# A mixture-of-experts block on one core: x1 formed on VectorE in its own step, its squares on ScalarE, the expert choice one step sooner

## What is computed

```python
x = x + layernorm(A(layernorm(x)))      # A: long convolution (S4D), below
x = x + layernorm(F(layernorm(x)))      # F: mixture of experts, below
```

```python
z = layernorm(x) * g + b
logits = z @ rW + rb                    # 8 experts
top 2 of softmax(logits) -> weights w
hid = gelu(z @ W1[e] + b1[e]);  out = hid @ W2[e] + b2[e]
return z_in + sum_e w[e] * out[e]
```

## Time and profile before

| | us |
|---|---|
| median of 3 runs | 642.32 (641.46 to 644.99) |
| the profiled execution | 644.5 |
| its span | 642.9 |

### The profile page before, as it was taken

One profiled execution on the slowest core, in us unless ns is written; L12 is line 12 of the kernel. 1 busy time (PEld: TensorE's weight loads), 2 busy tenths in 40 slices (PEclk: granted clock), 3 DMA queues, 4 the chain that ended last, 5 costly groups with the idle time before them and its releaser, 6 DMA issues. The chain is left out here.

```text
span 642.9 us, 12334 instructions
## 1 busy us (share of the span) xinstructions
PE 484.8 (75%) x2809; PEld 418.0 (65%) x2810; DVE 488.9 (76%) x1426; ACT 329.3 (51%) x646; POOL 262.4 (41%) x205
## 2 busy tenths in 40 slices
PE   0479899848997773600189999999999999992970
PEld 0239888736876663600078888888888889892760
DVE  7997959889988977884057778777777787770796
ACT  6974721353455366620055555555555555545485
POOL 0001586545776665788503223322332323233420
PEclk9998999968987985555579999999999999995995
DMA  6106500100110657642432222222222222215963
GB/s 198 66 0 262 197 1 0 66 1 9 59 68 33 229 197 216 227 139 74 153 118 68 81 66 82 66 82 66 82 67 80 66 82 72 75 49 212 346 229 145
DMA packets 36826, 69.55 MB, mean 108 GB/s; under 512 B 7520, under 2 KB 23648, under 8 KB 36160
## 3 DMA queue, kind: packets, MB, share of 16 engines
q1 hardware_dynamic: 30320, 51.48, 24.3%
q0 software_dynamic: 6480, 17.77, 7.7%
HBM read 42.02 MB, written 27.21 MB: 108 GB/s over the span
## 5 line engine op out<-in xcount | busy, mean ns | idle before, releaser
L1165 POOL DMA_INDIRECT y_rows<-y_sb,dst x71 | 76.6, 1079 | 192.7 <-DVE y_sb L1056 149.9
L1340 PE MATMUL psum<-ws,z_hl 128*128 x426 | 119.8, 417 | 0.8 <-DVE z_hl L1033 0.8
L1359 PE MATMUL psum<-ws,h_hl 128*128 x852 | 116.0, 286 | 0.1
L1359 PEld LDWEIGHTS psum<-ws,h_hl 128*128 128x128 f32 x852 | 103.6, 189 | 0.3 <-issue 0.3
L1147 POOL DMA_INDIRECT z_rows<-zn,pos x64 | 76.9, 1201 | 30.6 <-issue 17.7
L1340 PEld LDWEIGHTS psum<-ws,z_hl 128*128 128x128 f32 x426 | 76.7, 192 | 16.0 <-issue 1.5
L591 ACT CAST h_hl<-psum 128x512 fp32r<-128x512 f32 x71 | 41.7, 587 | 75.8 <-PE psum L1349 75.8
L1041 DVE TENSOR_TENSOR hb<-psum,b1r 128x512 f32<-128x512 f32 x71 | 49.1, 691 | 37.5 <-issue 34.0
L583 ACT ACTIVATE z_f<-psum,gb 128x128 f32<-128x128 f32 x142 | 57.0, 452 | 32.8 <-PE psum L1327 31.1
L1232 PE MATMUL psum<-pm,ft 128*128 128x256 f32 x256 | 65.7, 418 | 0.4 <-DVE tmp L836 0.4
L1327 PE MATMUL psum<-ident,z_in 128*128 128x128 f32 x142 | 28.6, 284 | 43.9 <-DMA z_in<-z_rows 42.0
(11 more groups left out here) (200 smaller groups left out, 874.7 us busy)
## 6 DMA issues: line engine op xcount, KB each, us to landing
z_in<-z_rows SPq DMA_DIRECT2D x71, 129.0 KB, 2.1
w_raw<-in_dram SPq DMA_DIRECT2D x16, 512.0 KB, 4.9
ya<-y_rows SPq DMA_DIRECT2D x16, 512.0 KB, 6.1
xs<-in_dram SPq DMA_DIRECT2D x8, 512.0 KB, 5.4
x_dram<-xs SPq DMA_DIRECT2D x8, 512.0 KB
x1m<-x_dram SPq DMA_DIRECT2D x2, 2048.0 KB, 8.4
out_dram<-acc SPq DMA_DIRECT2D x8, 512.0 KB, 2.6
b1r<-in_dram SPq DMA_DIRECT2D x8, 256.0 KB
```

Of the source, the lines that this page charges most:

```text
L1165: pool.indirect_dma_start(y_rows, bass.IndirectOffsetOnAxis(ap=dst[q][:, 0:1], axis=0), y_sb[q][:, :], None).then_inc(sem(f"y_out{q}"), 16)
L1340: last = TE.matmul(ps_h[q], z_hl[q][:, a, k], w_at(e1, c, k * F, F), start=n == 0, stop=n == 5)
L1359: last = TE.matmul(ps_y[q], h_hl[q][:, a, k], w_at(e2, c, 1024 + k * H, H), start=n == 0, stop=n == 11)
```

## The change

- x1 is made on VectorE in the step of its o: four instructions compute `o * rs + x` with an accumulator output that gives the sum of each token (its mean follows from it). The shift of o (`-mean*rs`, the same for all channels of a token) is not added to x1. It doesn't change the norm of x1; it is kept in `xb` and added in the mix, in one more small VectorE instruction per row. `dl` and GpSimd's addition go away.
- The variance of x1 comes from four ScalarE instructions (Square with the mean as bias and an accumulator output) in the same step, instead of `bn_stats` and `bn_aggr` on VectorE one step later. ScalarE then makes `zn` in the same step too, and copies the token numbers.
- `turn`, the logits and `choose` come one step sooner (row n-2); the ranks, `place` and the scatters stay with row n-3, and for the last rows row 6 is placed in step 8 beside row 5. `place` now stands behind r's statistics. The router bias and the experts' first rows are added by matmuls with the identity instead of on VectorE.
- GpSimd: `combine(row, 1)` moves to the start of the next step, `combine(row, 0)` waits for o, and the eight scatters of a row are issued as five and three around it. GpSimd makes no weight splits any more.
- The splits of the weights are spread over other steps; only that of expert 7 stays behind the tile table.
- SyncE writes the padding blocks before it waits for the last scatters.
- A one-element Gelu is put on ScalarE ahead of the tiles.

```diff
@@ SyncE
             behind = [sp.value_load(padi[0:1, e:e + 1], min_val=0, max_val=ROWS - P) for e in range(E)]
-            for i in (2, 3):
-                sp.wait_ge(sem(f"scattered{i}"), 128)
             for e in range(E):
                 sp.dma_start(z_rows[bass.ds(behind[e], P), :], zpad[:, :]).then_inc(sem("pads"), 16)
...
             sp.wait_ge(sem("pads"), 16 * E)
+            for i in (2, 3):
+                sp.wait_ge(sem(f"scattered{i}"), 128)
             load_z(0, 0)
@@ ScalarE
-            def renormalise(mid):
-
-                sigma(mid, 3)
-                act.wait_ge(sem("st_x1"), mid.b + 1)
+            def renormalise(row):
+
+                act.wait_ge(sem("x1_mean"), row.b + 1)
+                for k in range(4):
+                    last = nc.scalar.activation(dump[:, k], xs[row.b][:, k], ACT.Square, bias=mv1[:, row.b, k, 0:1],
+                                                accum_out=mv1[:, row.b, k, 1:2])
+                last.then_inc(sem("var3"), 1)
+                sigma(row, 3)
+                act.wait_ge(sem("st_x1"), row.b + 1)
...
+                elif row.b < 6:
+                    act.wait_ge(sem(f"scattered{row.par}"), 64 * (row.b - row.par))
...
+                nc.scalar.copy(zn[buf(row.b)][:, :, H], tok[:, row.b])
...
+                for e in HIGH.get(n, ()):
+                    split_high(e)
                 if cur.live:
-
                     sigma(cur, 1)
-                    act.wait_ge(sem("st_o"), cur.b + 1)
-                    if not cur.first():
-                        act.wait_ge(sem("x1_ready"), cur.b)
-                    for k in range(4):
-                        last = nc.scalar.activation(dl[:, k], o[:, k], ACT.Identity, bias=rs[:, 1, 4 + k:5 + k],
-                                                    scale=rs[:, 1, k:k + 1])
-                    last.then_inc(sem("dl_ready"), 1)
                 if inv.live:
...
-                if mid.live and n != B:
-                    renormalise(mid)
-                for e in HIGH.get(n, ()):
-                    split_high(e)
+                if cur.live:
+                    renormalise(cur)
@@ VectorE
                     stats(lambda k: r[:, k], 2)
+                if last_tail.live and n != B + 1:
+                    place(last_tail)
                 if cur.live:
                     do(inverse(cur, 2))
...
                 if n == B:
-                    mid_now()
+                    choose(tail)
...
                 if nxt.live:
                     mult(nxt, 1)
+                if n == B:
+                    place(tail)
                 if cur.live:
                     do(inverse(cur, 1))
-                    V.scalar_tensor_tensor(rs[:, 1, 4:8], mv[1][:, :, 0], -1.0, rs[:, 1, 0:4], ALU.mult,
+                    V.scalar_tensor_tensor(xb[:, cur.b], mv[1][:, :, 0], -1.0, rs[:, 1, 0:4], ALU.mult,
                                            ALU.mult).then_inc(sem("st_o"), 1)
...
+                    for k in range(4):
+                        last = V.scalar_tensor_tensor(xs[cur.b][:, k], o[:, k], rs[:, 1, k:k + 1], xs[cur.b][:, k], ALU.mult,
+                                                      ALU.add, accum_out=st[:, 3, 0, k:k + 1])
+                    last.then_inc(sem("x1_ready"), 1)
+                    dve.wait_ge(sem("x1_ready"), cur.b + 1)
+                    V.tensor_scalar(mv1[:, cur.b, :, 0], st[:, 3, 0, 0:4], -1.0 / H, None, ALU.mult).then_inc(sem("x1_mean"), 1)
                 for e in LOW.get(n, ()):
                     split_low(e)
...
+                if tail.live and n != B:
+                    choose(tail)
+                if cur.live:
+                    do(inverse(cur, 3))
+                    V.tensor_tensor(rs[:, 3, 4:8], mv1[:, cur.b, :, 0], rs[:, 3, 0:4], ALU.mult).then_inc(sem("st_x1"), 1)
@@ VectorE, mix
                 V.scalar_tensor_tensor(rm[:, par, 2, :], mvm[par][:, :, 0], -1.0, rm[:, par, 1, :], ALU.mult,
-                                       ALU.mult).then_inc(sem("m_rs"), 1)
+                                       ALU.mult).then_inc(sem("m_sh"), 1)
+                dve.wait_ge(sem("m_sh"), b + 1)
+                gate(dve)
+                V.tensor_tensor(rm[:, par, 2, :], rm[:, par, 2, :], xb[:, bass.ds(back(b), 1)].rearrange("p a k -> p (a k)"),
+                                ALU.add).then_inc(sem("m_rs"), 1)
@@ GpSimd
+                nxt, cur, tail, last_tail = (Row(n, k) for k in (1, 0, -2, -LAG))
+
+                if cur.live and cur.b:
+                    if cur.b > 1:
+                        pool.wait_ge(sem("st_x1"), cur.b - 1)
+                    combine(cur, 1)
+                if last_tail.live and n != B + 1:
+                    scatter(last_tail, 0, 5)
                 if nxt.live:
+                    if nxt.b > 1:
+                        pool.wait_ge(sem("o_ready"), nxt.b - 1)
                     combine(nxt, 0)
-                    combine(nxt, 1)
+                    if nxt.b == 0:
+                        combine(nxt, 1)
+                if last_tail.live and n != B + 1:
+                    scatter(last_tail, 5, 8)
+                if n == B:
+                    scatter(tail, 0, 8)
@@
-HIGH = {3: (0,), 4: (1,), 5: (2,), 6: (3,), 7: (4,), 9: (5,), 10: (6,)}
-LOW = {9: (0,), 10: (1,), B + LAG: (4, 5, 6, 7)}
-LOW_POOL = {B + LAG: (2, 3)}
+HIGH = {0: (0, 1), 1: (2,), 4: (3,), 7: (4,), 8: (5, 6)}
+LOW = {1: (0, 1), 2: (2,), 8: (3,), 9: (4, 5, 6), B + LAG: (7,)}
```

More of the change, by code:

```diff
@@ L879, in place @@
                 V.tensor_copy(zn[buf(row.b)][:, :, H + 1], mif[:, 1])
-                V.tensor_copy(pos[row.par][:, :, :], posr[:, :, :]).then_inc(sem("pos_ready"), 1)
+                with nc.allow_low_precision(reason="one term of each sum is not zero, and it is a whole number"):
+                    V.tensor_reduce(pos[row.par][:, :, :], prod[:, :, :, :], AX.X, ALU.add).then_inc(sem("pos_ready"), 1)
             def step(n):
-                nxt, cur, mid, tail = (Row(n, k) for k in (1, -1, -2, -LAG))
@@ L896, in mid_now @@
-                def mid_now():
-                    dve.wait_ge(sem("x1_ready"), mid.b + 1)
-                    for k in range(4):
-                        last = V.bn_stats(st[:, 3, k, :], xs[mid.b][:, k])
-                    do(last)
-                    mid_statistics()
-                    mid_scales()
+                nxt, cur, tail, last_tail = (Row(n, k) for k in (1, -1, -2, -LAG))
                 if cur.live:
@@ L1124, in fold, with scatter @@
                 G.tensor_tensor(pm[b][:, 1], xn[b % 3][:, 0:2], xn[b % 3][:, 2:4], ALU.subtract).then_inc(sem("pm_ready"), 1)
-            def split_low(e):
-                pool.wait_ge(sem("w_high"), e + 1)
-                G.tensor_tensor(ws[:, e, 1], w_raw[e][:, :], ws[:, e, 0].bitcast(F32), ALU.subtract).then_inc(sem("w_low"), 1)
-            def step(n):
-                nxt, cur, tail = (Row(n, k) for k in (1, -1, -LAG))
+            def scatter(row, lo, hi):
+                pool.wait_ge(sem("pos_ready"), row.b + 1)
+                for i in range(lo, hi):
+                    pool.indirect_dma_start(z_rows, bass.IndirectOffsetOnAxis(ap=pos[row.par][:, i // 4, i % 4:i % 4 + 1], axis=0),
+                                            zn[buf(row.b)][:, i % 4], None).then_inc(sem(f"scattered{buf(row.b)}"), 16)
@@ L1153, in _ @@
             steps(step)
-            for e in LOW_POOL[B + LAG]:
-                split_low(e)
             def scatter_y(t, q):
```

130 lines of the change are left out of this document (44 added, 86 removed).

## The result

The changed kernel takes 622.18 us (median of four runs, 619.58 to 627.88), the kernel before 643.65 beside it (641.46 to 645.51): a ratio of 0.968, 95% interval 0.960 to 0.976. Forecast were 620 us, range 607 to 634. The profiled execution (627.88 us, span 626.3) is the slowest of the four, so one more profile of the same kernel was taken (a2_changed, span 620.3), and both stand in this table. The marks were read from the timelines: start of r in step 3 and step 8 on VectorE, end of the last scatter on GpSimd, first transpose of a tile on TensorE, first addition of the mix on VectorE, end. In brackets is what the prediction gave, put on the times of before.

A forecast was written before the change was run, and what follows sets the result against it. VectorE was taken to bound the steps, and waits for scatters and padding the gap before the tiles. -25.0 us to the first tile and +2.4 in the mix gave -22.6 on 642.3: 619.7, say 620 us, range 607 to 634.

The forecast's parts named there:

- Part 1, VectorE's loop: Full steps, 3 to 6: VectorE's own chain, with its wait for ScalarE's root, takes 19.4 us against 22.2.
- Part 1, TensorE's loop: Full steps: 17.6 us of TensorE work plus half-clock loss and following work; both loops meet at 20.2, saving 8.1 over four.
- Part 2: First and last steps: step 3 begins 3.1 us later, step 7 takes 17.4, step 8 begins at 237.1.
- rival 2: Full steps: zn waits for scatters now started in the same step; if 3 us per step, +12, 632 us; chance 0.12.
- Part 3: Last scatters: sixteen with 11.9 us of stalls end at 288.8 against 305.53, -16.7; row 7's own path just inside.
- The stall rule: Scatters: a VectorE weight split stops GpSimd's descriptor work; one costs about 1.8 to 2.1 us, four in a row 8.65.
- Part 4: Gap before the first tile: padding lands before the last scatter, saving 8.3 us; first transpose at 293.3, -25.0 in all.
- Part 5: Mix: one more small VectorE instruction per row costs 0.3 us, eight rows +2.4; bounds +0.2 and +6.
- GpSimd's placing: Full steps: sums moved away from o's shift save 1.1 us per step, lost again if GpSimd is a microsecond late.
- x1 at half rate: x1's four VectorE instructions run at two cycles per element: 1.07 us more per step, +8, 628 us; chance 0.2.
- Padding not the last: Before the first tile: weight loads, b1 and b2 or the table come last, the 8.3 us stay: 628; chance 0.07.
- TensorE's clock slower than before: Full steps: TensorE stays at half clock, 39 us per step, +19 in each of four, about 695 us; chance 0.03.

The follow-up runs named there:

- e3_rank_later: Changed kernel with TensorE's rank matmuls moved between the two halves of the forward transform: 618.33 us, 0.963 of the kernel before.
- b1_pads_alone: Kernel before with only the padding blocks issued ahead of the wait for the last scatters: 635.24 us, 0.987 of the kernel before.
- e6_both: e3_rank_later with ScalarE's copy of s moved behind the squares and root of x1's variance: 616.40 us, 0.956 of the kernel before.
- e10_loads_later: e6_both with expert 5's weight load and the x1 stores behind it held until row 3's scatters landed: 612.96 us, 0.953 of the kernel before.
- s1_sums_back: Changed kernel with both GpSimd sums at once, without their waits, and all eight scatters behind them: 657.88 us, 1.023 of the kernel before.
- s2_no_waits: Changed kernel with its GpSimd order kept and only the sums' waits for o and x1's scales removed: 636.71 us, 0.991 of the kernel before.
- e8_fill_half: e6_both with unused identity matmuls in TensorE's idle stretches from step 7 to the first tile and before the mix: 614.36 us, 0.953.

## Why the prediction was right, by its steps

**The sum.** -22.6 was forecast on the profiled span; a2_changed ends at 620.3, -22.6, and after at 626.3, -16.6. The ratio of the medians gives -3.2%, 20.6 us, on 642.3. The range held all four runs. That a2_changed agrees to the tenth is luck, for several terms were off and cancelled. Against the forecast it has 2.9 us less in the first steps, 0.7 less in the four full ones, 2.1 more in step 7, 1.4 less to the last scatter, 0.9 more to the first tile, 0.6 more in the tiles and 1.6 more in the mix. Two sums of the prediction are off by a little as well: step 8's beginning adds up to 236.95 (237.1), and row 7's own path to +50.6 (+50.8).

**Part 1, VectorE's loop: right, 1.1 us too long.** Forecast were 19.4 us where VectorE alone sets the step. e3_rank_later shows it free of TensorE: 18.3. By the terms of the sum, read there: r 4.2 (taken 4.5), o 9.2 (9.6), shift 0.2 (0.1), x1 1.7 (1.7), mean 0.1 (0.3), choice 1.8 (1.8), wait and hops for the root 0.8 (1.1), scale 0.3 (0.3).

**Part 1, TensorE's loop: right in size, wrong in form.** It was said that TensorE would idle for the mask, that the matmuls behind would go at half clock, and that the step would settle at 20.2. The mean of four is 20.0 to 20.7, but it doesn't settle: long steps and short ones take turns, for a late TensorE hides its own wait a step later. Taking the wait off TensorE's head removes it (e3_rank_later). I had put the two loops side by side and taken a value between them; what the trace of before could have told is that the order of TensorE's queue, not its 17.6 us of work, made the second loop, and that more was to be had (6.7 us in the steps, 4.7 at the last scatter).

**Part 2: two misses.** Step 3 begins 3.2 us later in after, as forecast, but that is luck. From the beginning of step 1 to that of step 3 it takes 40.9 us in after, in a2_changed and in every experiment with the same first steps, against 39.6 before and 38.4 in b1_pads_alone; so steps 1 and 2 grew by 1.3 to 2.5 us, not 3.1, and the rest arose ahead of step 1, whose beginning lies between 95.1 and 98.3 us from run to run (98.1 in after). Step 7 was forecast 17.4, and is 19.5 to 19.7. What failed is that the 17.4 stood without TensorE's loop, which was worked out for steps 3 to 6 only: TensorE ends 16.4 us into it, and copy, squares and root come behind, 3.2 us more. The wait for scatters is there too (1.32 and 1.74 us), but off the path. It comes on it when the ranks are moved (3.37 us in e3_rank_later, 4.59 in e6_both), and in one place only, where SyncE's weight load and x1 stores run beside row 3's scatters; rival 2 had been priced for all full steps or none. With squares ahead of the copy and those transfers held back step 7 is 16.8 (e10_loads_later); the second alone wasn't tried. Step 8's chain held to a microsecond or so: choice at +11.8 (forecast +12.3), row 6's positions at +18.5 (+19.4), row 7's at +37.0 (+38.0).

**Part 3: right, for another reason.** The scatters end 50.3 us after step 8 begins in both profiles (forecast 51.7). I had them bound by GpSimd's queue with 11.9 us of stalls. They have 8.0 (the six long ones after row 6's positions in after, less 0.96 each), GpSimd has caught up and waits 3.75 us for row 7's positions, and then it is row 7's own path that ends last, the +50.8 that I called just inside. The stall rule held: 3.43 us under one split, 10.03 under four.

**Part 4: right.** 8.28 us on the old kernel; the gap of 12.8 is 5.4 to 5.6 in the changed one, against 4.5 forecast.

**Part 5: too low.** The mix grew by 3.8 (after) where 2.4 was taken, 0.43 per row for 0.3. The bare instruction is 0.16; I undersized the wait for its own engine's result (0.28).

**GpSimd's placing: undersized in the text.** It was booked as -1.1 per step for the shift, with GpSimd late by a microsecond as the danger. s1_sums_back shows that without it the change as a whole loses (1.023), and s2_no_waits that without its two waits 0.9% of the 3.2% are left: x1 on VectorE is what the sums would then stop, and zn in the step of x1 is what late scatters would stop.

**The rivals.** x1 at half rate (0.2) is refuted: 256 elements take 0.48 us, at a pitch of 0.41, and 0.08 for the accumulator is hidden in it; that is 1.74 for four, where half rate would have been 2.8. The rule of the Trainium skill's Vector Engine (DVE) Microarchitecture Reference ("Points that are easy to get wrong") isn't borne out by these rows. zn waiting for scatters (0.12) costs nothing in the changed kernel (1.32 us in step 7, off the path), and is real from step 4 on in s1_sums_back. Padding not the last (0.07) is refuted by b1_pads_alone. TensorE's clock slower than before (0.03): long steps at 0.86 and 0.88, short ones at 0.96, the old ones at 0.88; with the idle time before it, it cost some 2 us a step (20.0 to 20.7 against 18.3 in e3_rank_later) and not 19.

## What to carry to other kernels

When two engines hand a step to each other, look at what stands first in each queue, not only at the work in it: one small matmul group that waits for the other engine, at the head of TensorE's queue, cost 3 us of idle time and 3 more at half clock behind it. When work is moved onto VectorE, look where GpSimd's large sums will then lie, for one took 0.9 us and two took 2.8 us of the VectorE instruction beside them; and when a buffer is to be rewritten a step sooner, everything on the DMA engines beside its last reader counts. Behind the last matmul of a step, look at the queue of the engine that takes its result: work that doesn't need it belongs ahead of it. A gain that a profile promises at one wait (padding, 8.3 us) can be tried alone on the old kernel first.

## What the runs showed of the hardware

- ScalarE's accumulator read is 0.19 us, and four squares with it take 2.1 us, one every 0.49, no more than `dl`'s four without one (2.08).
- A scatter issued at the same time landed 3.6 us sooner without a 1 MB weight load and two x1 stores beside it (e6_both and e10_loads_later).
- After 2.89 us without work TensorE went on for ten microseconds, 6.2 of them busy, at 1.2 GHz (e8_fill_half); after 3.26 us its next 32 matmuls took 10.04 us for 7.15 (after).
- A VectorE instruction and GpSimd sums hold up each other or only one of the two: 3.31 us for 0.48 on VectorE under two sums that kept their 1.28 and 1.27 (s2_no_waits); where both engines had such instructions in a row, 2.17 for 1.23 on VectorE and 2.18 and 2.25 for 1.27 on GpSimd (s1_sums_back, from 150.75).
- From the end of the last scatter to the load that waited for it it took 3.0 to 3.9 us with eight padding blocks issued just ahead, and 2.0 to 2.5 without.
